# A third bank for scores, one bank for small jobs, and parts of maxima and tokens made by GpSimd, in a one-layer transformer kernel

## The chip, the cores and the metric

The kernel runs on one core of one Trainium2 chip. The metric is the device time of one execution in microseconds (us), lower is better. Several executions are timed and the median is given; one more execution is profiled.

## What is computed

The input x has 8 batches of 256 tokens of width 128 (2048 tokens). One layer in float32, normalised after each half:

```python
# attention: 16 heads of width 8
Q, K, V = proj(Wq, bq), proj(Wk, bk), proj(Wv, bv)
scores = einsum('bhqd,bhkd->bhqk', Q, K) / sqrt(8)
attended = einsum('bhqk,bhkd->bhqd', softmax(scores), V)
x = layernorm(x + attended @ Wo + bo)
# shared part (256 hidden) and 8 experts (128 hidden), the best 2 of 8 for each token
shared_out = (silu(xf @ sw1) * (xf @ sw3)) @ sw2
s = sigmoid(xf @ router_w.T)
_, topk_idx = top_k(s + router_bias, 2)      # gates: s of the chosen over their sum
routed_out = sum over the chosen e of gate_e * (gelu(xf @ ew1[e]) @ ew2[e])
x = layernorm(x + shared_out + routed_out)
```

## The kernel before

**Slots.** `lay_out_slots` writes the order of the work out by hand as a list of slots, and every engine runs through the same list, taking from each slot what is its own; semaphores tie the engines together. A slot holds up to one half-slot of scores (`s`), one of maxima (`m`), products with v (`pv`) and a list of small `jobs`. There are 14 slots of entry, 64 with scores, and a tail with 40 units. A batch takes eight half-slots; maxima run 12 slots ahead of scores.

**Attention.** In each half-slot TensorE makes the scores of two heads' tiles, keys by queries, for `r` = 0 and 1 (`scores`, L800), and the same products the other way round for two other tiles (`maxima`, L809). Scores and maxima use different 32-row groups of the array and are issued by turns. VectorE reduces each maxima bank to the largest score of each query (`top`, L672; three banks `max_bank`). When a batch's eight half-slots are reduced, `top` is negated and split in a high and a low part (`top_parts`, L681 and L682), TensorE transposes them (job "shift", L893, one slot later), ScalarE copies them (L618) and sends them by DMA (L621) into spare rows of `qstack`, so that the scores of that batch come out with the maximum subtracted. ScalarE takes the exponential of each scores bank (L570), TensorE multiplies with v (L826), and ScalarE copies the result (L578).

**Projections.** Queries and keys come in units of 512 tokens. The jobs "k" and "q" of unit n are a matmul (L882), two copies on ScalarE (L607, L611), a subtraction on GpSimd (L486), and 12 DMA copies each ("store", L371). "v" is L885. Unit 0 is made in another way in the entry (jobs "first").

**The small jobs of a batch.** "norm" (transposes L901, divided by the sums on VectorE, L702 and L703), "attT" (L907, copied by ScalarE, L624), "wo" (L912, added and its statistics taken on VectorE, L711 to L718), "y" (normalised on GpSimd, L496 to L499), "yT" (L918; ScalarE makes the high part `yt_hi`, L626, VectorE the low part `yt_lo`, L722), "router" (six small matmuls, exponential L630). Every second batch the group of 512 tokens is routed: route0 to route5 on GpSimd, with "sig", "rank" and "den" (L732 to L734) on VectorE between them, then "combT" (transposes L931, copy L636, DMA to scratch) and "load gates" (a DMA that spreads 2 MB to `gates_mem`). On GpSimd also stand "add bo" (L492) and 16 pieces of "split w" (L468, L470).

**The tail.** Unit u is three matmuls of 512 columns (L780 to L782), an activation (L643 or L645), a product with the gates (L750) or two for a shared unit (L742, L745), and two slots later the second matmul "down" (L960).

**PSUM banks.** There are eight of 512 columns: `ring` x2 (scores and units, used by turns), `max_bank` x3, `pv_bank`, `misc_bank` and `sum_bank`. Small jobs take `misc_bank` and `sum_bank` by turns:

```python
            banks = ([misc_bank, sum_bank] if n < tail else [misc_bank, max_bank[2]] if n < tail + 3
                     else [misc_bank, pv_bank, max_bank[2]] if n < tail + 14 else [misc_bank, pv_bank])
```

`wait_ring` makes TensorE wait, before it writes a ring bank, for the exponential of the bank's last use; `wait_bank` and `wait_taken` make it wait for the engine that reads a small job's bank.

## Time and profile before

| | |
|---|---|
| median of 3 runs | 232.85 us (232.33 to 233.04) |
| profiled execution, its own time | 230.98 us |
| its span, first to last instruction | 229.2 us |
| TensorE busy | 207.9 us, 91% of the span |
| VectorE busy | 157.3 us, 69% |
| ScalarE busy | 137.9 us, 60% |
| GpSimd busy | 107.5 us, 47% |
| mean granted TensorE clock | 0.974 of full |

The shares are means over stages with different limits: up to about 30 us the entry, to 121.5 us scores beside maxima, to 141 us scores alone, then the units. The lines named are those of the kernel before. PE is TensorE's matmuls, PEld its weight loads, DVE VectorE, ACT ScalarE, POOL GpSimd, SP the queue that issues most DMAs.

### The profile page before, as it was taken

The numbers are of one execution on the slowest core, as the hardware profiler recorded it, in microseconds if no ns is written. First come the engines' busy times: TensorE is split into PE (matmuls) and PEld (weight loads), VectorE is DVE, ScalarE is ACT, GpSimd is POOL, SyncE is SP. The second block draws the span as 40 slices with busy tenths as digits, with TensorE's granted clock in tenths as the row PEclk, the third lists the DMA queues.
The fourth block names the chain that finished last, engine by engine and source line by source line (L and its number), as shares of the span: only waits on it lengthen the run. The fifth ranks groups of instructions, "written<-read, shape, count | busy, mean of one in ns | idle before, by whom it ended". The sixth has DMA issues, their size and how long they took to land.

```text
span 229.2 us, 4496 instructions
## 1 busy us (share of the span) xinstructions
PE 207.9 (91%) x1538; PEld 120.0 (52%) x1538; DVE 157.3 (69%) x333; ACT 137.9 (60%) x280; POOL 107.5 (47%) x208
## 2 busy tenths in 40 slices
PE   7998979989998989999899999899998999999970
PEld 7764555435564645546454554466664455645520
DVE  6688877849899899989994030664548655556654
ACT  2899464878877778778778877334341533534330
POOL 8787997023506379582965156144003802020203
PEclk9999955999999999999999999999999999999998
DMA  4391654384410000009000350000090010541011
GB/s 154 107 258 31 167 166 104 99 307 104 103 27 6 3 6 4 9 3 366 10 3 6 140 233 0 3 1 0 3 366 0 3 47 1 182 186 46 3 44 48
DMA packets 10422, 19.19 MB, mean 84 GB/s; under 512 B 1952, under 2 KB 7008, under 8 KB 9760
## 3 DMA queue, kind: packets, MB, share of 16 engines
q1 hardware_dynamic: 8976, 17.06, 22.7%
q10 hardware_dynamic: 1040, 1.05, 1.3%
q0 software_dynamic: 384, 0.79, 1.3%
q8 instruction: 13, 0.21, 0.4%
q14 instruction: 9, 0.07, 0.1%
HBM read 12.80 MB, written 1.11 MB: 61 GB/s over the span
## 4 chain that ended last, share of the span: by engine, by line
PE 68%; DVE 18%; ACT 7%; issue 4%; ACTq 1%; POOL 0%; POOLq 0%; DVEq 0%
PE ring L800 14%; PE pv_bank L826 10%; PE max_bank L960 9%; DVE top L672 8%; PE sum_bank L960 4%; PE ring L782 3%; PE ring L780 3%; PE ring L781 3%; ACT probs_mem L570 3%; PE max_bank L809 3%; PE pv_bank L834 2%; DVE hid L750 2%; PE misc_bank L882 1%; ACT xt L645 1%; PE misc_bank L780 1%
## 5 line engine op out<-in xcount | busy, mean ns | idle before, releaser
L672 DVE TENSOR_REDUCE top<-max_bank 128x2 f32<-128x512 f32 x128 | 81.0, 682 | 10.7 <-PE max_bank L809 10.4
L570 ACT ACTIVATE probs_mem<-ring 128x512 f32<-128x512 f32 x128 | 70.0, 596 | 19.4 <-PE ring L800 17.8
L800 PE MATMUL ring<-qstack,kstack 32*128 32x256 f32 x256 | 45.5, 336 | 6.4 <-ACT probs_mem L570 3.7
L809 PE MATMUL max_bank<-kstack,qstack 32*128 32x256 f32 x256 | 44.4, 338 | 1.1 <-DVE top L672 0.8
L800 PEld LDWEIGHTS ring<-qstack,kstack 32*128 32x128 f32 x256 | 29.3, 190 | 27.1 <-ACT probs_mem L570 16.1
L826 PE MATMUL pv_bank<-probs_mem,v 128*18 128x256 f32 x512 | 41.4, 397 | 0.4 <-ACT probs_mem L570 0.4
L750 DVE TENSOR_TENSOR hid<-xt,gates_mem 128x512 f32<-128x512 f32 x32 | 22.5, 703 | 24.0 <-ACT xt L645 24.0
L645 ACT ACTIVATE xt<-ring 128x512 f32<-128x512 f32 x32 | 19.1, 598 | 32.4 <-PE ring L782 32.4
L960 PE MATMUL max_bank<-hid,wf 128*128 128x512 f32 x60 | 32.0, 614 | 1.7 <-DVE hid L750 1.4
L809 PEld LDWEIGHTS max_bank<-kstack,qstack 32*128 32x128 f32 x256 | 28.3, 190 | 5.9 <-POOL kstack L475 1.8
L780 PE MATMUL ring<-yt_hi,wf_lo 128*128 128x512 f32 x40 | 31.3, 782 | 0.0
L505 POOL TENSOR_SCALAR rstd<-mv 128x4 f32<-128x4 f32 (+1 forms) x5 | 1.9, 388 | 36.9 <-DVE mv L764 36.8
L782 PE MATMUL ring<-yt_hi,wf_hi 128*128 128x512 f32 x40 | 15.8, 395 | 0.0
L781 PE MATMUL ring<-yt_lo,wf_hi 128*128 128x512 f32 x40 | 15.8, 394 | 0.0
L826 PEld LDWEIGHTS pv_bank<-probs_mem,v 128*18 128x18 f32 x512 | 8.7, 97 | 9.9 <-issue 1.0
L960 PEld LDWEIGHTS max_bank<-hid,wf 128*128 128x128 f32 x60 | 9.6, 188 | 7.8 <-DVE hid L750 5.9
L486 POOL TENSOR_TENSOR gates_mem<-gates_mem 128x512 fp32r<-128x512 f32 x6 | 7.6, 1270 | 12.9 <-ACT gates_mem L611 12.9
L643 ACT ACTIVATE xt<-ring 128x512 f32<-128x512 f32 x8 | 4.8, 597 | 14.6 <-PE pv_bank L782 5.6
L499 POOL TENSOR_SCALAR xs<-res,mv,rstd 128x128 f32<-128x128 f32 x16 | 12.7, 802 | 0.9
L780 PEld LDWEIGHTS ring<-yt_hi,wf_lo 128*128 128x128 f32 x40 | 7.6, 190 | 9.5 <-issue 8.4
L781 PEld LDWEIGHTS ring<-yt_lo,wf_hi 128*128 128x128 f32 x40 | 7.6, 190 | 9.1 <-issue 9.1
L742 DVE SCALAR_TENSOR_TENSOR xt<-xt,ring 128x512 f32<-128x512 f32 x8 | 5.5, 688 | 9.1 <-ACT xt L643 9.1
(191 smaller groups left out, 333.2 us busy)
## 6 DMA issues: line engine op xcount, KB each, us to landing
gates_mem<-gate_scratch SPq DMA_DIRECT2D x4, 2048.0 KB, 7.2
kstack<-gates_mem SPq DMA_DIRECT2D x36, 64.0 KB, 2.1
qstack<-gates_mem SPq DMA_DIRECT2D x24, 64.0 KB, 2.1
wf<-w_ffn_dram SPq DMA_DIRECT2D x1, 1408.0 KB, 6.3
xs<-x_dram SPq DMA_DIRECT2D x4, 256.0 KB, 5.4
xt<-x_t_dram SPq DMA_DIRECT2D x3, 256.0 KB, 4.4
qstack<-gates_mem POOLq DMA_DIRECT2D x12, 64.0 KB, 2.3
out_dram<-xs SPq DMA_DIRECT2D x3, 256.0 KB, 2.3
```

The source lines that it names most:

```text
L499: ins = pool.tensor_scalar(xs[:, QT * n + t, :], res1[:, t, :], mv1[:, t, 0:1], rstd1[:, t:t + 1], ALU.subtract, ALU.mult)
L570: nc.scalar.activation(probs[:, i % 2, s_heads(s)[r], :], ring_of(("scores", 2 * s + r))[:, :], ACT.Exp, scale=SCALE).then_inc(probs_made, 1)
L645: nc.scalar.activation(act_out[:, b % 2, :], bank[:, :], ACT.Gelu).then_inc(act_made, 1)
L672: dve.tensor_reduce(top[:, m_heads(m)[r], t, :], max_bank[(2 * m + r) % NMAX][:, :].rearrange("p (h k) -> p h k", h=2), AX.X, ALU.max).the ...
L750: dve.tensor_tensor(hid[:, b % NHB, :], act_out[:, b % 2, :], gates_mem[:, g % 2, e * GT:(e + 1) * GT], ALU.mult).then_inc(hid_dve, 1)
L780: mm(out_ap, w_lo, m_hi, start=first, stop=False)
L781: mm(out_ap, w_hi, m_lo, start=False, stop=False)
L782: return mm(out_ap, w_hi, m_hi, start=False, stop=last)
L800: ins = mm(ring_of(("scores", 2 * s + r))[:, kt * S:(kt + 1) * S], kstack[rows, t, k:k + P], qstack[rows, t, b * S:(b + 1) * S], start=Tru ...
L809: ins = mm(max_bank[(2 * m + r) % NMAX][:, qt * S:(qt + 1) * S], qstack[rows, t, q:q + P], kstack[rows, t, b * S:(b + 1) * S], start=True, ...
L826: ins = mm(pv_bank[32 * j:32 * j + 2 * VW, 0:S], v[:, (QT * b + kt) * H // 2 + HPS * n + j, k * VW:(k + 2) * VW], probs[:, p // 2 % 2, j, ...
L960: mm(acc_bank[g][:, :], wf[:, c:c + P], hid[:, b % NHB, :], start=b == first_of(g), stop=b == last_of(g)).then_inc(down_made, 1)
```

## The change

1. **Scores in three banks.** Scores take `ring[0]`, `ring[1]` and `sum_bank` in turn. Units still take the two ring banks.
2. **Small jobs in one bank.** While there are scores, every small job uses `misc_bank`, and the layout spreads the jobs over slots of their own: "wo" goes a slot behind the shift, the router is cut in two jobs ("router0", "router") five and six slots later than before, "k", "q" and "v" of later units are moved.
3. **Parts of the maxima on GpSimd.** A job "tops", at the front of the slot in which a batch's last maxima are made, does with three operations what VectorE did with two. `top` has two copies.
4. **Parts of the tokens on GpSimd.** ScalarE copies the transposed tokens to `yt_raw`, GpSimd makes `yt_hi` and `yt_lo` from it; VectorE's L722 is gone.
5. **"combT" once for a group** (four transposes in one bank, one wider copy, one DMA). The second group's moves from slots 54 and 55 of the scores to the tail's first. The last group's routing starts one slot later (12 + n for 11 + n); its "combT" stays at 24.
6. **The third unit's queries** (unit 2) stand in slot 12 of the entry, before 13.
7. `hid`, the units' product, takes the place of half of the probabilities in SBUF.

```diff
@@ lay_out_slots
-                   (10, ("v", 0)), (11, ("k", 2)), (12, ("split rw", 0)), (13, ("q", 2))):
+                   (10, ("v", 0)), (11, ("k", 2)), (12, ("q", 2)), (12, ("split rw", 0))):
...
-    put(4, ("v", 2))
-    for n, job in ((8, ("k", 3)), (9, ("store", (3, 1))), (10, ("q", 3)), (12, ("store", (3, 0))), (13, ("v", 3))):
+    for n, job in ((2, ("v", 2)), (7, ("k", 3)), (8, ("store", (3, 1))), (15, ("q", 3)), (16, ("store", (3, 0))), (16, ("v", 3))):
...
+    for slot in slots:
+        if slot.m is not None and slot.m % 8 == 7:
+            slot.jobs.insert(0, ("tops", slot.m // 8))
...
-        for kind, n in (("norm", 2), ("attT", 3), ("wo", 4), ("y", 5), ("yT", 8)):
+        for kind, n in (("norm", 2), ("attT", 3), ("wo", 5), ("y", 6), ("yT", 9)):
             put(first + n, (kind, b))
         if b < NB - 2:
-            put(first + 9, ("router", b))
+            put(first + 14, ("router0", b))
+            put(first + 15, ("router", b))
         if b % 2:
             for kind, n in route:
-                put(first + 9 + n, (kind, b // 2))
+                put(first + 15 + n, (kind, b // 2))
             if b // 2 < 2:
-                put(first + 22, ("combT", b - 1))
-                put(first + 23, ("combT", b))
-                put(first + 25, ("load gates", b // 2))
+                put(first + 32, ("combT", b // 2))
+                put(first + 34, ("load gates", b // 2))
...
     for kind, n in route:
-        put(NHALF + 11 + n, (kind, NG - 1))
+        put(NHALF + 12 + n, (kind, NG - 1))
@@ banks
-            banks = ([misc_bank, sum_bank] if n < tail else [misc_bank, max_bank[2]] if n < tail + 3
+            banks = ([misc_bank, sum_bank] if n < first_s else [misc_bank] if n < tail else [misc_bank, max_bank[2]] if n < tail + 3
...
+                if use[0] == "scores":
+                    bank, n_scores = (ring + [sum_bank])[n_scores % 3], n_scores + 1
+                else:
+                    bank, n_units = ring[n_units % 2], n_units + 1
+                ring_of[use], ring_before[use], ring_latest[bank.name] = bank, ring_latest.get(bank.name), use
@@ GpSimd
+                    if kind == "tops":
+                        pool.wait_ge(max_taken, 16 * (n + 1))
+                        if n >= 2:
+                            pool.wait_ge(misc_made, made["shift", n - 2])
...
+                        chain(pool.tensor_scalar(hi, tops, -1.0, None, ALU.mult))
+                        chain(pool.tensor_scalar(tops, tops, -1.0, None, ALU.mult))
+                        pool.tensor_tensor(lo, tops, hi.bitcast(F32), ALU.subtract).then_inc(top_split, 1)
...
+                    if kind == "yT":
+                        wait_taken(pool, (kind, n))
+                        c = slice(n * S, (n + 1) * S)
+                        chain(pool.tensor_scalar(yt_hi[:, c], yt_raw[:, n % 2, :], 1.0, None, ALU.mult))
+                        pool.tensor_tensor(yt_lo[:, c], yt_raw[:, n % 2, :], yt_hi[:, c].bitcast(F32), ALU.subtract).then_inc(yt_made, 1)
@@ VectorE
-                    if m % 8 == 7:
-                        dve.wait_ge(max_taken, 2 * m + 2)
...
-                        chain(dve.tensor_scalar(hi, tops, -1.0, None, ALU.mult))
-                        dve.scalar_tensor_tensor(out=lo, in0=tops, scalar=-1.0, in1=hi.bitcast(F32), op0=ALU.mult,
-                                                 op1=ALU.subtract).then_inc(top_split, 1)
...
-                    if kind == "yT":
-                        dve.wait_ge(yt_hi_made, b + 1)
-                        dve.tensor_tensor(yt_lo[:, b * S:(b + 1) * S], misc[:, 0:S],
-                                          yt_hi[:, b * S:(b + 1) * S].bitcast(F32), ALU.subtract).then_inc(misc_dve, 1)
```

How the program stands before and after is shown in three places; a row is a source line, the instruction and its output and inputs. The new file's lines are numbered otherwise.

TensorE at the end of the entry, before; L882 to `misc_bank` is the third unit's queries, L800 the first scores:

```order
L809 MATMUL max_bank<-kstack,qstack 128x256 x4
L882 MATMUL sum_bank<-xt,wa 128x512
L809 MATMUL max_bank<-kstack,qstack 128x256 x8
L882 MATMUL misc_bank<-xt,wa 128x512
L800 MATMUL ring<-qstack,kstack 128x256
```

TensorE in the same place after, up to the second half-slot of scores (L896 was L882, L811 was L800, L820 was L809):

```order
L896 MATMUL sum_bank<-xt,wa 128x512
L820 MATMUL max_bank<-kstack,qstack 128x256 x4
L896 MATMUL misc_bank<-xt,wa 128x512
L820 MATMUL max_bank<-kstack,qstack 128x256 x4
L811 MATMUL ring<-qstack,kstack 128x256
...
L811 MATMUL sum_bank<-qstack,kstack 128x256
```

The queries' matmul has moved in front of four maxima, and the third scores bank is `sum_bank`.

GpSimd behind the DMA issues of the entry, before (L486 is the low part of keys or queries, L492 the addition of bo):

```order
L371 DMA qstack<-gates_mem 32x512 x12
L486 TENSOR_TENSOR gates_mem<-gates_mem 128x512
L461 TENSOR_SCALAR rw_parts<-rw 128x8
L462 TENSOR_TENSOR rw_parts<-rw,rw_parts 128x8
L486 TENSOR_TENSOR gates_mem<-gates_mem 128x512
L492 TENSOR_TENSOR xs<-xs,bo_all 128x512 x4
```

GpSimd in the same place after:

```order
L377 DMA qstack<-gates_mem 32x512 x12
L499 TENSOR_TENSOR gates_mem<-gates_mem 128x512 x2
L474 TENSOR_SCALAR rw_parts<-rw 128x8
L475 TENSOR_TENSOR rw_parts<-rw,rw_parts 128x8
L505 TENSOR_TENSOR xs<-xs,bo_all 128x512
L469 TENSOR_SCALAR top_parts<-top 128x4x8
L470 TENSOR_SCALAR top<-top 128x32
L471 TENSOR_TENSOR top_parts<-top,top_parts 128x4x8
L505 TENSOR_TENSOR xs<-xs,bo_all 128x512 x2
```

The parts of the second batch's maxima stand between the first addition and the next two.

TensorE around the shift of a batch in the middle, before:

```order
L826 MATMUL pv_bank<-probs_mem,v 18x256 x4
L893 MATMUL sum_bank<-ident,top_parts 32x128 x2
L912 MATMUL misc_bank<-wa,att_t 128x128 x2
L800 MATMUL ring<-qstack,kstack 128x256
L809 MATMUL max_bank<-kstack,qstack 128x256
```

The same place after, up to "wo":

```order
L837 MATMUL pv_bank<-probs_mem,v 18x256 x4
L907 MATMUL misc_bank<-ident,top_parts 32x128 x2
L811 MATMUL ring<-qstack,kstack 128x256
L820 MATMUL max_bank<-kstack,qstack 128x256
...
L837 MATMUL pv_bank<-probs_mem,v 18x256 x4
L926 MATMUL misc_bank<-wa,att_t 128x128 x2
```

The shift stands alone in its slot, and "wo" comes a slot later.

## Rows read from the trace of the kernel before

**Rows 1.** the page's first line, and TensorE's clock granted in 40 equal slices (tenths)
```profile
span 229.2 us, 4496 instructions
...
PEclk9999955999999999999999999999999999999998
```

**Rows 2.** windows of five stages: length, busy us (count) by engine, clock, DMA share, GB/s
```profile
29.30:39.60 10.30, 9.20 (x67) 5.49 (x68) 7.83 (x13) 5.83 (x12) 9.36 (x11) 0.51 0.48 127
39.60:54.50 14.90, 13.87 (x144) 6.71 (x144) 10.65 (x20) 11.98 (x24) 2.54 (x2) 1.00 0.60 185
54.50:121.50 67.00, 63.77 (x748) 35.58 (x746) 62.48 (x138) 52.61 (x112) 38.43 (x88) 1.00 0.15 50
121.50:141.00 19.50, 18.25 (x175) 9.54 (x171) 4.29 (x18) 14.93 (x33) 10.91 (x27) 1.00 0.27 111
141.00:229.20 88.20, 77.58 (x282) 45.20 (x280) 49.47 (x119) 32.17 (x58) 21.00 (x44) 0.99 0.17 61
```

**Rows 3.** groups by line, 54.5 to 121.5 us: busy, mean ns | idle before, releaser
```profile
L672 DVE TENSOR_REDUCE top<-max_bank 128x2 f32<-128x512 f32 x80 | 50.4, 680 | 1.5 <-PE max_bank L809 1.2
L570 ACT ACTIVATE probs_mem<-ring 128x512 f32<-128x512 f32 x79 | 43.4, 596 | 12.7 <-PE ring L800 11.4
...
L722 DVE TENSOR_TENSOR yt_lo<-sum_bank,yt_hi 128x256 fp32r<-128x256 f32 x5 | 2.1, 424 | 2.1 <-ACT yt_hi L626 2.1
...
L523 POOL TENSOR_SCALAR tie<-diff 128x256 f32<-128x256 f32 x2 | 1.7, 861 | 0.2
```

**Rows 4.** tile top_parts: duration ns min/median/max, first and last start
```profile
L681 DVE TENSOR_SCALAR top_parts<-top x8: 181/182/576, 21.8 to 121.1; 128x32 fp32r<-128x32 f32 x8
L682 DVE SCALAR_TENSOR_TENSOR top_parts<-top,top_parts x8: 191/192/1210, 22.3 to 121.4; 128x32 fp32r<-128x32 f32 x8
```

**Rows 5.** timeline around the shift of one batch: start us, us, instruction
```profile
66.40 0.68 DVE L672 TENSOR_REDUCE top<-max_bank 128x2 f32<-128x512 f32 x1
...
67.34 0.19 DVE L682 SCALAR_TENSOR_TENSOR top_parts<-top,top_parts 128x32 fp32r<-128x32 f32 x1
...
67.67 0.38 PE L893 MATMUL sum_bank<-ident,top_parts 128*32 128x128 f32 x2
```

**Rows 6.** timeline of the entry into the scores, 22 to 30 us
```profile
22.62 0.38 PE L893 MATMUL misc_bank<-ident,top_parts 128*32 128x128 f32 x2 [0.66 <-DVE top_parts L682]
...
28.77 0.68 ACT L611 ACTIVATE gates_mem<-misc_bank,wa 128x512 f32<-128x512 f32 x1
29.34 1.08 ACT L570 ACTIVATE probs_mem<-ring 128x512 f32<-128x512 f32 x2
...
30.00 0.58 PE L800 MATMUL ring<-qstack,kstack 32*128 32x256 f32 x1 [1.40 <-DVE top L672]
```

**Rows 7.** the chain that ended last, in order of time: start us, us, what
```profile
38.41 1.54 PE sum_bank L885 x8
...
47.08 0.68 ACT gates_mem L611
...
85.77 0.56 PE pv_bank L826 x8
87.29 0.56 PE pv_bank L826 x8
```

**Rows 8.** ACT's groups by line, 121.5 to 141 us
```profile
L570 ACT ACTIVATE probs_mem<-ring 128x512 f32<-128x512 f32 x24 | 13.1, 596 | 3.4 <-PE ring L800 3.0
```

**Rows 9.** timeline of the last group's routing, 190 to 193 us
```profile
190.06 0.23 POOL L537 TENSOR_SCALAR den_ok<-den 128x4 f32<-128x4 f32 x1 [2.79 <-DVE den_inv L734]
190.08 0.80 PE L780 MATMUL ring<-yt_hi,wf_lo 128*128 128x512 f32 x1
...
191.73 0.79 PE L780 MATMUL ring<-yt_hi,wf_lo 128*128 128x512 f32 x1
191.88 0.25 POOL L546 TENSOR_TENSOR comb<-picked,mask 128x32 f32<-128x32 f32 x1
...
192.83 0.38 PE L931 MATMUL misc_bank<-ident,comb 128*8 128x128 f32 x2
```

113 lines of the change are left out of this document (60 added, 53 removed).

## The prediction

> **What bounds the kernel now.** I read five stages first [rows 2]. From 54.5 to 121.5 us, where every slot makes one half-slot of scores, one of maxima and one product with v, VectorE is busy for 62.48 of 67.00 us, TensorE for 63.77 and ScalarE for 52.61. [...] Inside the stage [rows 3] the 80 reductions sit idle for only 1.5 us, and the piece of VectorE's time that is waste is 2.1 us in front of five yt_lo subtractions, which wait for ScalarE's yt_hi. ScalarE waits 11.4 us for scores: two ring banks make TensorE and ScalarE take turns. So VectorE is the bound here, with the turn-taking close behind. From 121.5 to 141 us there are no maxima; ScalarE is busy for 14.93 of 19.5 us and waits 3.0 us for scores [rows 2, 8]: the two banks are the limit there. From 141 us on are the 40 units, TensorE 77.58 of 88.2 us [rows 2]; a unit's slot costs 191.73 - 190.08 = 1.65 us [rows 9]. One more place stands out: the granted clock is 0.51 of full from 29.3 to 39.6 us, the lower of its two levels, and 1.00 or near it in the other four stages [rows 1, 2]. It fell while TensorE had just sat idle for 1.40 us at the entry into the scores [rows 6], behind ScalarE's two copies of the third unit's queries (28.77 + 0.68) and the first exponentials at 29.34.
>
> **The base of the sum.** The profiled execution took 230.98 us, 1.78 more than its span of 229.2 [rows 1]; the median shown is 232.85, so 1.87 above it. I make the sum against 230.98 and put it on the median unchanged.
>
> **Entry, 20 to 30 us.** The parts of the maxima of batch 0 go to GpSimd. The wait of TensorE before that shift was 0.66 us [rows 6]; I take GpSimd's step from six chained small operations, 190.06 to 191.88 + 0.25, so 2.07 / 6 = 0.345 us each [rows 9], and three of them are 1.04 against 0.18 + 0.19 and about 0.1 of chaining on VectorE [rows 4]. That is 0.6 us more in front of the shift, and some 0.2 for its place in GpSimd's queue: +0.8. Against it, the queries' matmul now stands before the last lone maxima, so ScalarE's two copies (0.68 each [rows 6]) end before the first scores rather than after them, and the second half-slot of scores finds the third bank free instead of waiting for an exponential. Of the 1.40 us of idle time almost all goes: -1.4. Together -0.6. Bounds: +0.8 (the copies are late anyway) and -1.4.
>
> **Clock, 29.3 to 39.6 us.** Four slots, bo, one v (1.54 us at the low level [rows 7]) and one shift fill 9.9 us. At full clock, slots in the middle of the kernel stand 87.29 - 85.77 = 1.52 us apart [rows 7], the v costs half of 1.54 to all of it, say 1.1, bo and shift 0.5 together: 4 x 1.52 + 1.6 = 7.7, a gain of 2.2 if the clock holds. I think it does, since the idle time that preceded the fall goes away. If it falls in the same place all the same, what is left is the shift there: VectorE's two parts took 0.58 and 1.21 us, the longest of their kinds [rows 4], beside GpSimd's additions; three GpSimd steps and half of one addition in its queue ahead of them (0.6) are about as long, so 0 to -0.8. The Trainium skill (TensorE: Matmul & The Clock Gate, "What's actually happening") says that the low level is the default and recent activity is what releases it. By that rule a fuller entry keeps the clock, which is the -2.2; the trace agrees in that the fall followed the idle time, but it shows four busy slots at the low level too, which the rule alone does not explain.
>
> **39.6 to 54.5 us.** The fourth unit's queries leave this stage for slot 15. Their two copies on ScalarE are 2 x 0.68, and the chain ran through such a copy at 47.08 [rows 7]: -1.4. The third bank covers some of the keys' copies: -0.2. Together -1.6, bounds 0 (they only move on) and -2.5.
>
> **54.5 to 121.5 us, five batches.** Removed from VectorE per batch: 0.18 + 0.19 + 0.42 = 0.79 us of work [rows 3, 4], 3.95 in all, and the 2.1 us of waits before yt_lo. That leaves 67.0 - 3.95 - 2.1 = 60.95. Given back: in the batch shown the last reduction ended at 66.40 + 0.68 = 67.08, VectorE's second part at 67.53, and TensorE came to the shift at 67.67, having waited for nothing [rows 5]. GpSimd will have them at 67.08 + 0.05 + 1.04 = 68.17, so TensorE stands 0.5 us, and VectorE, which then runs out of maxima, with it: 5 x 0.5 = 2.5. The later queries and v put some 0.3 here. 60.95 + 2.8 = 63.8: -3.2. Bounds: -6.05 (cover holds) and 0. GpSimd pays per batch three small steps (1.04) and two passes over 128x256; the nearest row for such a pass is 0.86 us [rows 3], so at most 1.04 + 1.72 = 2.8, or 14 us on top of 38.43 of 67 [rows 2]. That is 78% busy, and the tokens' parts are wanted only five slots later, so I cost them at nothing; if the cover goes, a batch costs up to 1.7 us. One bank for all small jobs costs nothing as long as each job's copy is done one slot (1.5 us) later, which copies of 0.4 to 0.7 us allow.
> The Trainium skill (SBUF — State Buffer, "SBUF: two separate sides") speaks against moving work to GpSimd: a GpSimd operation and a VectorE operation that reads two SBUF tensors exclude each other. Here the second part, which reads two, stretched from 0.19 to 1.21 us once [rows 4]. By that rule the new GpSimd work would slow VectorE, but the reductions read one tensor, in PSUM, so by rule and row alike the sum stays.
>
> **121.5 to 141 us.** Of the 3.0 us that ScalarE waits for scores [rows 8] the third bank takes 2.2, since TensorE can then make one exponential's scores ahead; what stays is behind small jobs. -2.2, bounds 0 and -3.4.
>
> **141 us on.** The last group's routing is put one slot later, its transposes are not. Before, the weights were ready at 191.88 + 0.25 = 192.13 and TensorE reached the transposes at 192.83: 0.70 us of slack [rows 9]. A slot is 1.65 us, so TensorE will wait 0.95. The second group's four transposes come into this stage; a pair takes 0.38 [rows 9], so +0.45 with overlap. Their wider copy stands before the first unit's activation: +0.3. Together +1.7, bounds +0.4 and +2.7.
>
> **Sum.** -0.6 - 2.2 - 1.6 - 3.2 - 2.2 + 1.7 = -8.1. 230.98 - 8.1 = 222.9 for the profile, 232.85 - 8.1 = 224.8 for the median.
>
> **Rivals.** (1) The clock falls all the same. GpSimd's parts make a wait of about 0.66 + 0.8 = 1.5 us before batch 0's shift, as long as the idle time that preceded the fall before. In the same place it costs 1.4 us of the sum, 226.2; earlier, up to 3 more, 229. Against it: the two idle pieces of before (0.66 and 1.40) become one. (2) The freed VectorE buys little, because the single bank and GpSimd's queue tie the engines together: the stage with maxima gives 0.5, the one after it 1.0, the tail costs 2.5, the rest as summed (-0.6 - 2.2 - 1.0): -2.8, or 230.0. For it speaks that TensorE too is shown 63.77 of 67. (3) Slower: the parts of the maxima come out of GpSimd's queue so late that TensorE stands long in every batch. It decides from about 1.7 us a batch on, since seven batches x (1.7 - 0.5) eat the 8.1, or from 1.3 us if such a wait makes the clock fall once more (2.2). Behind the two passes of the tokens' parts it would be 1.72 and, with one fall, 232.85 - 8.1 + 7 x 1.22 + 2.2 = 235.5. Against it: the tokens' parts stand two slots ahead in GpSimd's order. (4) Nothing changes: gains in the maxima stage only lengthen waits elsewhere, 232.8.
>
> **Chances.** The sum as it stands 0.50 (its own range 222.5 to 226.5), (1) 0.25, (2) 0.13, (4) 0.04, (3) 0.08. About 0.3% is what a measurement of this kernel can tell from no change. Faster 0.88, same 0.04, slower 0.08. The range goes from 221.5, where VectorE's cover holds, to 230.5, which takes in (1) and (2).
>
> **What would show it.** Right: granted clock 1.00 from 29 to 40 us; VectorE busy near 58.5 in a stage of about 64 us, TensorE waiting some 0.5 us before each shift; ScalarE's wait for scores after the maxima under 1 us; TensorE idle for 1 us before the last group's transposes. Wrong: a low clock stretch of the same or greater length; waits before the shift over 1.5 us; a stage after the maxima still at 19 us, which would mean that TensorE's own time was its limit.

## The result, and the profile after

The changed kernel is slower. Its median is 242.33 us (235.80 to 244.08, 6 executions), that of the kernel before 232.84 us (232.28 to 233.38, 6 executions): 9.5 us, or 4.1%, more. The forecast was 224.8, with a range of 221.5 to 230.5.

Executions of one and the same kernel differ in how long TensorE's granted clock stays at its lower level; left to the executions with the least of it, the ratio is still 1.019 (interval 1.0127 to 1.0252). To compare kernels I take from every execution its time at the low level, 2 x (1 - granted clock) x span. In 14 further executions of the kernel before, a straight line through the times rises by 0.33 us for each us at the low level, and passes 10 us at 230.7. The six of the changed kernel have 19.6 to 51.3 us of it. Their line, extended down to 10 us, where none of them lies, gives 233.9, which is 3.2 more. Set beside single executions of the kernel before with as much of it, the changed kernel is 2 to 3 us slower where both have 19 to 23 us, and 0.3 to 1.1 us slower where both have 44 us. So of the 9.5 us **some 3 at most are there at an equal clock**, and the rest comes with more time at the low level (44 us in the middle executions, about 16 in those of before).

The page of the changed kernel, its first line and the granted clock in 40 slices, to be held against [rows 1]:

```profile
span 242.2 us, 4497 instructions
...
PEclk9999959999999998557999555599999999999996
```

One low stretch has become three. The windows of the same kernel (columns as in [rows 2]) are cut at the shifts of successive batches; the first is the idle time before the shift at 95.21, the last three are the last shift to the first unit, the low stretch that begins in it, and the units:

```profile
93.80:95.20 1.40, 0.11 (x4) 0.02 (x1) 0.72 (x2) 0.48 (x1) 1.15 (x5) 0.97 0.00 0
68.12:81.33 13.21, 12.26 (x149) 6.71 (x150) 11.69 (x23) 10.12 (x22) 8.24 (x18) 1.00 0.04 13
81.33:95.21 13.88, 12.26 (x148) 6.70 (x149) 11.94 (x24) 10.13 (x22) 9.75 (x24) 1.00 0.01 4
95.21:113.78 18.57, 18.36 (x149) 8.88 (x149) 12.21 (x27) 10.11 (x22) 13.66 (x33) 0.54 0.01 3
127.34:152.99 25.65, 25.39 (x174) 12.53 (x175) 4.06 (x16) 14.01 (x30) 12.28 (x26) 0.60 0.09 35
132.80:156.60 23.80, 23.80 (x141) 11.36 (x142) 3.19 (x12) 13.40 (x28) 7.26 (x17) 0.50 0.03 8
152.99:242.20 89.21, 79.16 (x284) 46.30 (x282) 50.13 (x118) 32.92 (x57) 30.07 (x59) 0.96 0.22 83
```

The kernel before, cut at the same places:

```profile
67.67:80.97 13.30, 12.57 (x153) 6.96 (x150) 12.39 (x27) 10.44 (x23) 6.12 (x13) 1.00 0.01 4
80.97:94.33 13.36, 12.59 (x150) 6.99 (x149) 12.67 (x30) 10.41 (x23) 11.14 (x26) 1.00 0.01 4
94.33:108.32 13.99, 13.22 (x156) 7.22 (x153) 12.85 (x29) 11.01 (x25) 7.47 (x19) 1.00 0.39 153
121.70:140.98 19.28, 18.03 (x172) 9.49 (x171) 4.12 (x16) 14.73 (x32) 10.89 (x27) 1.00 0.27 113
140.98:229.20 88.22, 77.60 (x282) 45.22 (x281) 49.47 (x119) 32.17 (x58) 21.02 (x44) 0.99 0.17 61
```

The two batches that both kernels ran at full clock took 13.21 and 13.88 us after, 13.30 and 13.36 before. VectorE's work did fall, from 12.39 to 11.69 us in a batch, and bought 0.09 us in one and -0.52 in the other. The batch from 95.21 us took 4.6 us more than its counterpart and the stage after the maxima 6.4 more; those are the places with a clock of 0.54 and 0.60.

What took VectorE's gain are the waits of TensorE for the parts of the maxima. Around an ordinary shift (timeline; to be held against [rows 5]):

```profile
80.07 0.63 PE L837 MATMUL pv_bank<-probs_mem,v 128*18 128x256 f32 x8
80.18 0.29 POOL L469 TENSOR_SCALAR top_parts<-top 128x32 fp32r<-128x32 f32 x1 [0.74 <-DVE top L692]
80.56 0.29 POOL L470 TENSOR_SCALAR top<-top 128x32 f32<-128x32 f32 x1
80.93 0.25 POOL L471 TENSOR_TENSOR top_parts<-top,top_parts 128x32 fp32r<-128x32 f32 x1
81.33 0.38 PE L907 MATMUL misc_bank<-ident,top_parts 128*32 128x128 f32 x2 [0.63 <-POOL top_parts L471]
82.20 0.69 DVE L692 TENSOR_REDUCE top<-max_bank 128x2 f32<-128x512 f32 x1 [0.90 <-PE max_bank L820]
```

And around the one at which the clock fell, where GpSimd was in the middle of a group's routing:

```profile
92.94 1.04 POOL L534 TENSOR_TENSOR diff<-sel 128x64 f32<-128x64 f32 x4
94.07 0.29 POOL L469 TENSOR_SCALAR top_parts<-top 128x32 fp32r<-128x32 f32 x1
...
94.81 0.25 POOL L471 TENSOR_TENSOR top_parts<-top,top_parts 128x32 fp32r<-128x32 f32 x1
...
95.21 0.59 PE L907 MATMUL misc_bank<-ident,top_parts 128*32 128x128 f32 x2 [1.30 <-POOL top_parts L471]
...
96.59 0.69 DVE L692 TENSOR_REDUCE top<-max_bank 128x2 f32<-128x512 f32 x1 [2.07 <-PE max_bank L820]
```

In the first, GpSimd starts behind the last reduction it needs and takes three steps of 0.37 to 0.4 us. In the second nothing waits in front of L469: GpSimd comes to it from four `diff` operations, and the wait doubles. The wait at the entry is 1.54 us, the last shift's 0.94. The transpose at 95.21 already runs at the low level: its two take 0.59 us, 0.38 at 81.33. The list of waits (engine, line, releaser: total us, times, longest):

```profile
PE misc_bank L907 <- POOL top_parts L471: 6.5, 8, 1.5
...
PE pv_bank L948 <- POOL comb L564: 1.6, 1, 1.6
...
DVE top L692 <- PE max_bank L820: 22.4, 34, 2.4
```

VectorE's wait for maxima has grown from 10.4 us in the kernel before to 22.4. In the two batches at full clock it is 1.4 and 1.2 us, where it was 0.3 and none: the bank that VectorE empties is filled later, because the shift stands in TensorE's order ahead of the next maxima. In the batch at the low clock it is 5.3 us, with TensorE itself slower.

### The profile page after: what moved, and what is told of

The parts are those of the page before. It is cut to its first block, busy times and chain, and to the rows that moved or that the text cites. A ratio compares the mean times of both kernels' runs of the same rounds, so it can differ in the third digit from the quotient of the medians.

```text
span 242.2 us, 4497 instructions
## 1 busy us (share of the span) xinstructions
PE 219.4 (91%) x1538; PEld 123.2 (51%) x1538; DVE 152.2 (63%) x309; ACT 137.2 (57%) x276; POOL 128.5 (53%) x248
## 4 chain that ended last, share of the span: by engine, by line
PE 62%; ACT 13%; DVE 12%; POOL 6%; issue 5%; ACTq 1%; POOLq 0%; DVEq 0%
PE pv_bank L837 12%; PE max_bank L979 8%; PE ring L811 6%; DVE top L692 5%; PE sum_bank L979 4%; ACT probs_mem L588 3%; PE ring L789 3%; PE ring L791 3%; PE ring L790 3%; PE sum_bank L811 3%; ACT probs_mem L616 3%; ACT probs_mem L613 2%; PE pv_bank L845 2%; PE misc_bank L915 2%; DVE probs_mem L759 1%
## 5 line engine op out<-in xcount | busy, mean ns | idle before, releaser
L692 DVE TENSOR_REDUCE top<-max_bank 128x2 f32<-128x512 f32 x128 | 81.3, 684 | 22.5 <-PE max_bank L820 22.4
L588 ACT ACTIVATE probs_mem<-ring 128x512 f32<-128x512 f32 x86 | 49.3, 601 | 19.9 <-PE sum_bank L811 9.4
L837 PE MATMUL pv_bank<-probs_mem,v 128*18 128x256 f32 x512 | 48.1, 454 | 2.0 <-ACT att_raw L596 1.7
L759 DVE TENSOR_TENSOR probs_mem<-xt,gates_mem 128x512 f32<-128x512 f32 x32 | 23.3, 728 | 31.9 <-ACT xt L665 31.9
L820 PE MATMUL max_bank<-kstack,qstack 32*128 32x256 f32 x256 | 41.5, 353 | 0.7 <-DVE top L692 0.4
L811 PE MATMUL ring<-qstack,kstack 32*128 32x256 f32 x172 | 40.3, 372 | 1.2 <-DVE top L692 1.1
L979 PE MATMUL max_bank<-probs_mem,wf 128*128 128x512 f32 x60 | 32.1, 616 | 1.7 <-DVE probs_mem L759 1.4
L811 PEld LDWEIGHTS ring<-qstack,kstack 32*128 32x128 f32 x172 | 24.9, 217 | 12.0 <-ACT probs_mem L588 5.5
L588 ACT ACTIVATE probs_mem<-sum_bank 128x512 f32<-128x512 f32 x42 | 25.1, 599 | 7.5 <-PE ring L811 6.1
L820 PEld LDWEIGHTS max_bank<-kstack,qstack 32*128 32x128 f32 x256 | 26.1, 201 | 6.0 <-POOL kstack L488 1.9
L811 PE MATMUL sum_bank<-qstack,kstack 32*128 32x256 f32 x84 | 24.1, 372 | 0.2 <-DVE top L692 0.2
L811 PEld LDWEIGHTS sum_bank<-qstack,kstack 32*128 32x128 f32 x84 | 14.6, 216 | 6.3 <-issue 3.6
L518 POOL TENSOR_SCALAR yt_hi<-yt_raw 128x256 fp32r<-128x256 f32 x8 | 6.9, 856 | 19.4 <-ACT yt_raw L646 19.4
L979 PEld LDWEIGHTS max_bank<-probs_mem,wf 128*128 128x128 f32 x60 | 9.6, 188 | 8.1 <-DVE probs_mem L759 6.0
L512 POOL TENSOR_SCALAR xs<-res,mv,rstd 128x128 f32<-128x128 f32 x16 | 13.1, 826 | 0.9
```

The costliest lines, as they stand in the source:

```text
L512: ins = pool.tensor_scalar(xs[:, QT * n + t, :], res1[:, t, :], mv1[:, t, 0:1], rstd1[:, t:t + 1], ALU.subtract, ALU.mult)
L588: nc.scalar.activation(probs[:, i % 2, s_heads(s)[r], :], ring_of["scores", 2 * s + r][:, :], ACT.Exp, scale=SCALE).then_inc(probs_made, 1)
L692: dve.tensor_reduce(top[:, b % 2, m_heads(m)[r], t, :], max_bank[(2 * m + r) % NMAX][:, :].rearrange("p (h k) -> p h k", h=2), AX.X, ALU.m ...
L759: dve.tensor_tensor(hid[:, b % NHB, :], act_out[:, b % 2, :], gates_mem[:, g % 2, e * GT:(e + 1) * GT], ALU.mult).then_inc(hid_dve, 1)
L811: ins = mm(ring_of["scores", 2 * s + r][:, kt * S:(kt + 1) * S], kstack[rows, t, k:k + P], qstack[rows, t, b * S:(b + 1) * S], start=True, ...
L820: ins = mm(max_bank[(2 * m + r) % NMAX][:, qt * S:(qt + 1) * S], qstack[rows, t, q:q + P], kstack[rows, t, b * S:(b + 1) * S], start=True, ...
```

## The experiments

Twelve kernels were run, and three more for a point that was open. All made from the changed kernel except e2. The numbers of all of them, with the time at the low level of each execution and, where the executions spread enough, where their line passes 10 us:

```
kernel                              median   low-level us of each        at 10 us   ratio to before
before, beside e1 to e4 (14)        233.12   11.9 to 44.6                230.7
before, beside e5 to e8 (7)         233.89   12.4 to 40.7                230.6
before, beside e9 to e12 (7)        232.10   11.9 to 19.0                230.1
before, beside e13 to e15 (7)       233.08   16.1 to 40.7                230.7
changed                             242.33   19.6 23.1 44.2 44.3 51.3 x2   233.9    1.019 (1.013-1.025)
e1 parts of maxima on VectorE       231.89   11.8 x2, 34.6 x2            227.5      0.980 (0.971-0.989)
e2 before, parts on GpSimd          236.68   8.4 to 41.5 (10 executions) 235.1      1.012 (1.006-1.018)
e3 changed, matmuls before shifts   240.44   7.4 27.2 28.6 31.7          234.4      -
e4 e1, parts of tokens on VectorE   229.22   8.6 9.5 13.6, 34.2 x2       228.6      0.982 (0.972-0.992)
e5 changed, shift a slot later      238.54   14.1 29.4 49.2 49.4         228.1      -
e6 e1, two matmuls in 12 slots      231.81   10.1 x2, 11.1 13.0          231.5      1.000 (0.990-1.009)
e7 e1, last routing a slot sooner   226.69   9.4 x2, 9.9, 33.0           226.7      0.975 (0.966-0.984)
e8 e1, two banks for scores         239.34   17.8 35.5 38.0 38.1         234.1      -
e9 e7, matmuls at the entry         227.08   9.5 9.9 11.7, 32.9          226.6      0.979 (0.972-0.985)
e10 e9, one matmul in 12 slots      228.08   8.6 x2, 9.0 11.8            228.3      0.985 (0.979-0.990)
e11 e7, shift a slot later          235.16   15.4 35.6 x2, 39.1          227.4      -
e12 parts on GpSimd, shift later    234.87   6.3 32.1 34.1 x2            227.8      -
e15 e12, one matmul in 12 slots     231.11   10.4 14.2 17.0 18.0         228.9      0.987 (0.977-0.998)
```

A dash stands where no ratio was formed. The extra matmuls of e3, e6, e9, e10, e12, e14 and e15 write into a bank before its real contents are made, or into one that is idle, so they change only the time, and so does the repeated reduction of e13. The slopes of the lines that the column at 10 us is read from lie between 0.20 and 0.40 us for each us; e6, whose four executions lie between 10.1 and 13.0 us, is read at 10.1 instead.

That column is an estimate of unequal worth. The changed kernel, e5, e8, e11 and e15 have no execution as low as 10 us, so their lines are extended, and e11's fits its four points only within some 2 us. Where it can be had, a batch at full clock between two shifts is the better measure:

```
                                    near 66 to 81 us, near 80 to 95 us
before                              13.30             13.36
changed                             13.21             13.88
e8 two banks for scores             13.24             13.19
e4 all parts on VectorE             13.11             13.21
e11 maxima's parts on VectorE,
    shift later                     12.93             12.92
e1, e7 maxima's parts on VectorE    12.90             12.86, 12.87
e5, e12 parts on GpSimd,
    shift later                     12.70             12.69
```

### e1, e2: the parts of the maxima alone

The theory: GpSimd's parts hold TensorE before each shift. The rival: the new layout and the single small bank do it. e1 puts the parts back on VectorE in the changed kernel, e2 moves only them in the kernel before.

```diff
@@ e1, VectorE; the job "tops" is gone from GpSimd's list
+                    if m % 8 == 7:
+                        dve.wait_ge(max_taken, 2 * m + 2)
+                        if b >= 2:
+                            dve.wait_ge(misc_made, made["shift", b - 2])
...
+                        chain(dve.tensor_scalar(hi, tops, -1.0, None, ALU.mult))
+                        dve.scalar_tensor_tensor(out=lo, in0=tops, scalar=-1.0, in1=hi.bitcast(F32), op0=ALU.mult,
+                                                 op1=ALU.subtract).then_inc(top_split, 1)
```

> The changed kernel with the parts of the maxima made by VectorE again (two operations behind a batch's last reduction), all else as changed. Theory A (GpSimd's late parts make TensorE stand 0.6 to 1.5 us before each shift, VectorE idles behind it, and the granted clock falls): no wait before a shift over 0.3 us, low clock only in one stretch of about 7 to 10 us at the entry, 226 to 229 us. Rival B (the third bank and the single bank for small jobs do it: small jobs wait on one bank, and the clock falls for that): waits before the other small jobs stay, low clock still 30 us or more, 234 us or more.

> The kernel before with nothing but the parts of the maxima moved to GpSimd. A: waits of 0.5 us or more before the shifts, more low clock than the one stretch of 10.2 us, 236 us or more. B: GpSimd's parts are harmless, 231 to 234 us and one low stretch.

At 10 us of low clock e2 rose from 230.7 to 235.1, both with executions there: in the old layout the move costs 4.4 us. But four of its ten executions have only 8.4 to 8.9 us at the low level, and take 234.6 to 235.0, so it costs that much without one more fall of the clock, which I had not expected. In the new layout e1 is at 227.5, 6.4 us below the extended line of the changed kernel; against the changed kernel's own two executions at 19.6 and 23.1 us of low clock it is 5 to 6. Without the move the rest of the change is worth about 3 us. Windows between shifts of e1, then of e2:

```profile
65.59:78.49 12.90, 12.61 (x149) 7.00 (x150) 12.02 (x26) 10.23 (x23) 7.63 (x15) 1.00 0.05 14
78.49:91.35 12.86, 12.62 (x148) 6.98 (x149) 12.24 (x27) 10.17 (x23) 7.63 (x17) 1.00 0.02 4
```

```profile
68.86:82.57 13.71, 12.56 (x148) 6.94 (x149) 12.01 (x26) 10.37 (x22) 6.97 (x17) 1.00 0.01 4
82.57:97.00 14.43, 12.79 (x148) 7.08 (x149) 12.44 (x29) 10.45 (x22) 11.97 (x30) 1.00 0.01 4
```

Half of e1's executions had some 23 us more at the low level, which was not expected either. In the profiled one that is a stretch from 124.3 to 148.2 us, behind the maxima, so the shifts are not the only place where the clock falls.

### e3: keep TensorE busy while it waits

```diff
@@ TensorE, before the shift of each batch
+                        for _ in range(5):
+                            mm(misc[:, 0:P], ident[:, :], ident[:, :], start=True, stop=True)
                         pe.wait_ge(top_split, b + 1)
```

> The changed kernel with five extra 128-column matmuls of the identity into the small jobs' bank in front of each shift (some 1.1 us of TensorE work that is overwritten), so that TensorE works while GpSimd makes the parts. A, with the clock as the main price: the low stretches after the entry go or shrink to under 10 us in all, 230 to 234 us. If the waits cost by themselves and the clock fell for another reason: low clock as in the changed kernel (about 48 us), 242 us or more.

No shift waits any more, and the profile has no low stretch at the entry or at the shifts, where the changed kernel had two. But the five take 1.38 us in a place where the wait was 0.63, and the batches took 13.74 and 13.80 us. At 10 us of low clock e3 is at 234.4, no better than the changed kernel's 233.9, and its median, 240.44, is far above the 230 to 234 expected, since the stretch behind the maxima stayed. It ties the first two clock falls to idle time of TensorE, and gains nothing.

```profile
PEclk9999999999999999999998555699999999999996
```

### e4, e8: the tokens' parts, and the third bank

```diff
@@ e8
-                    bank, n_scores = (ring + [sum_bank])[n_scores % 3], n_scores + 1
+                    bank, n_scores = ring[n_scores % 2], n_scores + 1
```

> The changed kernel with the parts of maxima and of tokens both on VectorE as before: third bank, single bank, layout, one combT and earlier queries alone. A: 227 to 230 us, within 1.5 us of the kernel with only the maxima's parts back, one low stretch. B: 234 us or more with several low stretches.

> The kernel with the maxima's parts on VectorE, and scores in the two ring banks by turns again; layout, single bank and the tokens' parts as changed. If the third bank gives the gain: 230 us or more at about 10 us of low clock, ScalarE waiting over 10 us for scores in the stage with maxima. If the removed VectorE work gives it: 227 to 228.5 us. If the third bank is also what makes the stage without maxima fall to the low clock, no run has the long stretch.

Tokens' parts back on VectorE cost 1.1 us (228.6 against 227.5; a batch takes 13.11 against 12.90, the next 13.21 against 12.86): that move was right. Scores in two banks, in this layout, cost 5.5 us in the execution with 17.8 us of low clock and 2.4 to 3.3 us in those with 35 to 38, against e1's line; the 6.6 us between the two lines at 10 us (234.1 against 227.5) come from extending e8's. A batch at full clock takes 0.33 us longer (13.24 against 12.90). ScalarE's wait for scores from 54.5 to 121.5 us is 11.4 us there, and 6.9 + 2.6 behind both kinds of bank in e1. So the third bank is a part of the change that earns something. It is not the cause of the clock falling behind the maxima either: e8 has that stretch too.

### e5: the shift one slot later

```diff
-        slot = next(n for n in range(len(slots)) if slots[n].m == 8 * b + 7) + 1
+        slot = next(n for n in range(len(slots)) if slots[n].m == 8 * b + 7) + 2
...
-        for kind, n in (("norm", 2), ("attT", 3), ("wo", 5), ("y", 6), ("yT", 9)):
+        for kind, n in (("norm", 2), ("attT", 3), ("wo", 4), ("y", 5), ("yT", 9)):
```

> The changed kernel with the shift one slot later and wo in the slot that the shift had; the parts stay on GpSimd. If only the wait before the shift matters (A), the waits there fall under 0.2 us in most batches, a batch takes 13.0 us or less instead of 13.2 to 13.9, and the time at about 10 us of low clock is near the 227.5 us of the kernel with the parts on VectorE (226 to 229). If work on GpSimd costs in another way (VectorE or ScalarE slowed by it), it stays at 232 us or more at that much low clock.

The waits before all shifts but the entry's (1.51) are gone, and the parts are still on GpSimd. The batches take 12.70 and 12.69 us, where the changed kernel took 13.21 and 13.88, and the extended line gives 228.1 at 10 us. That is the strongest single evidence: it is not GpSimd's work itself that costs, but that its reader stands only one slot behind it. The median, 238.54, is still bad, because the low stretches stayed. One begins at 103.9 us, 1.5 us after a wait that did not come from a shift:

```profile
100.83 0.25 POOL L552 TENSOR_TENSOR picked<-mask,sig 128x32 f32<-128x32 f32 x1
...
101.12 0.19 DVE L739 TENSOR_REDUCE den<-picked 128x4 f32<-128x32 f32 x1 [2.48 <-POOL picked L552]
...
102.44 0.35 PE L811 MATMUL ring<-qstack,kstack 32*128 32x256 f32 x1 [1.30 <-DVE top L692]
```

The routing on GpSimd is late, since it also makes the parts of the tokens and of wf, VectorE stands 2.48 us in its in-order list for it, the maxima behind it are not reduced, and TensorE stands 1.30 us. Whether this wait makes the clock fall is not shown: e8 and e11, with the maxima's parts on VectorE and no wait over 0.8 us there, have a stretch of 3.4 us from about 107 us too.

### e6, e9, e10: the clock

e6 adds two 128-column matmuls to each of the 12 slots in which scores stand without maxima; e9 adds three before the shifts of batches 0 and 1; e10 has those and one in each of the 12 slots.

```diff
@@ e6 with range(2), e10 with range(1)
+                if s is not None and m is None:
+                    pe.wait_ge(max_taken, 2 * NHALF)
+                    for _ in range(2):
+                        mm(max_bank[0][:, 0:P], ident[:, :], ident[:, :], start=True, stop=True)
@@ e9
+                        for _ in range(3 if b < 2 else 0):
+                            mm(misc[:, 0:P], ident[:, :], ident[:, :], start=True, stop=True)
```

> The kernel with the maxima's parts on VectorE, and two extra 128-column matmuls of the identity into an idle maxima bank in each of the 12 slots with scores and no maxima. If TensorE's light work there is what lets the clock fall (the stretch of 23.9 us from about 120 us on), no such stretch in any run, all runs within 1 us of each other, 226.5 to 229 us. If the clock falls for another reason, the stretch stays in about half of the runs and the median is 230 us or more.

> Parts of maxima on VectorE, last routing one slot sooner, and three 128-column identity matmuls ahead of the shift of the first two batches only, where TensorE stood 0.68 and 0.70 us. If the short stretch at the low clock at the entry (6.8 us in the profile of the kernel without these matmuls) hangs on those waits, it goes, and at 0.33 us for each us at the low clock the time falls by about 2 us, to 224.5 to 225.5 in the executions without the long stretch. If it hangs on something else, the time stays at 226.2 to 227, and executions near 234 come as before.

> The same with one further matmul in each of the 12 slots in which the scores stand alone. If one is enough to keep the clock there, all executions lie within 1 us of each other, with no long stretch, at 225 to 228 (two in each slot cost about 3.5 us). If one is too little, executions of 232 to 236 with a stretch of over 20 us at the low clock come up again.

With extra matmuls behind the maxima no execution of e6 (4), e10 (4) or e15 (4) has the long stretch; without them it comes in 2 of 4 (e1), 2 of 5 (e4), 1 of 4 (e7), 1 of 4 (e9), told by some 23 us more at the low level. The stage took 17.85 us in e7 and 19.83 in e10 at full clock, so one matmul a slot costs 2.0 us, and two cost about 4. With that e6 missed the 226.5 to 229 us expected, though the clock held. e7 then e10:

```profile
119.61:137.46 17.85, 17.34 (x175) 9.52 (x175) 3.95 (x16) 13.78 (x31) 11.47 (x25) 1.00 0.13 51
```

```profile
119.57:139.40 19.83, 19.56 (x197) 11.54 (x197) 3.94 (x16) 14.32 (x31) 11.61 (x26) 1.00 0.14 55
```

e9 is a miss for my theory of the entry: the waits of 0.68 and 0.70 us are gone and the stretch of 6.8 us came all the same; the time, 226.6 at 10 us of low clock, is that of e7. e3, with five matmuls before every shift, did not have it. Nor is the length of one wait enough: the changed kernel stood 1.54 us before the shift at 23.91, longer than the 1.40 us after which the clock fell in the kernel before, and ran at full clock until 30.4. What triggers the fall at the entry stays open.

### e7: the last routing one slot sooner

```diff
-        put(NHALF + 12 + n, (kind, NG - 1))
+        put(NHALF + 11 + n, (kind, NG - 1))
```

> The kernel with the maxima's parts on VectorE and the last group's routing one slot sooner, as before the change. The wait of 1.6 us before the last group's transposes goes; 1 to 1.6 us less at equal low clock, so 225.9 to 226.5 us at about 10 us of it. Rival: that wait only gives TensorE's time to the next one, under 0.3 us less.

The wait for the last group's gates (1.6 us in e1 too) is gone, and 0.8 us of it reaches the end: 226.7 against 227.5. This has the lowest median: 226.69 us, 0.975 of the kernel before (0.966 to 0.984), just above the 225.9 to 226.5 expected; e9, at 227.08, cannot be told from it. e10 is 1.4 us above it but has all four executions between 227.77 and 228.71, partly above the 225 to 228 expected.

### e11, e12, e15: GpSimd again, with the shift later

e11 is e7 with the shift later as in e5. e12 is the changed kernel with the shift later, the last routing sooner and five matmuls before the shift; the text of its expectation says before each shift, but the kernel run has them only before those of the first two batches. e15 is e12 with one matmul in each of the 12 slots.

> Parts of maxima on VectorE, last routing one slot sooner, and the shift one slot later (the output matmul takes its place). If the remaining waits of TensorE before the shift (0.68, 0.70 and 0.31) matter, they go, and the time is 225 to 226.5 in the executions without the long stretch. If VectorE's chain sets the batches' time, it is 226.2 to 227, or above, since the second part of the chain now starts later.

> Parts of maxima on GpSimd as in the changed kernel, the shift one slot later, the last routing one slot sooner, and five 128-column matmuls ahead of each shift. If all that GpSimd's parts cost is the wait that they put before the shift, this comes out with the kernels that have them on VectorE: 226.5 to 229 at 10 us of low clock. If GpSimd's own time is the cost (its queue, the routing behind it), it stays above 231.

> Parts of maxima on GpSimd, the shift one slot later, the last routing one slot sooner, five identity matmuls ahead of the first two batches' shifts, and one in each of the 12 slots in which the scores stand alone. If GpSimd's parts cost nothing once the shift comes later, and one matmul a slot keeps the clock after the maxima, all executions lie between 226 and 230 us. If the stretch at the low clock near 105 us, seen in both kernels with a later shift, is followed by a long one all the same, executions near 235 come up.

At 10 us of low clock e11 is at 227.4, a loose reading, and e12 at 227.8, with ten matmuls more. The batches at full clock tell them apart, e11 first:

```profile
68.52:81.45 12.93, 12.38 (x152) 6.77 (x148) 12.01 (x26) 10.00 (x23) 7.41 (x14) 1.00 0.01 4
```

```profile
67.18:79.88 12.70, 12.42 (x153) 6.80 (x149) 11.70 (x24) 10.06 (x23) 8.24 (x17) 1.00 0.02 6
```

With the shift later, the parts on GpSimd are the better place: VectorE has 0.31 us less to do, and the batch is 0.23 us shorter. At the end nothing of it is seen, since e12's stretch near 106 us (6.8 us at the low level) is longer than e11's (3.4). e12's best execution (226.62, 6.3 us at the low level) is among the fastest of all. e11 missed the 225 to 226.5 expected, and three of its four executions and three of e12's have the long stretch. e15 held the clock behind the maxima, as expected, and came out at 228.84 to 232.27, partly above the 226 to 230 expected: a stretch of 3.4 us near 106 us, behind the late routing, is still there.

### e13, e14: which engine sets the batch

The prediction took VectorE for the bound of the stage with maxima. Both kernels are e5 plus work on one engine alone; each was run once, for its profile (243.28 and 239.39 us, with long low stretches in both), and only a batch at full clock is compared.

```diff
@@ e13, VectorE: one reduction of each batch is made twice
+                        if b < 8 and m % 8 == 3 and r == 0:
+                            chain(dve.tensor_reduce(top[:, b % 2, m_heads(m)[r], t, :],
...
@@ e14, TensorE, before "wo"
+                        for _ in range(2):
+                            mm(misc[:, 0:P], ident[:, :], ident[:, :], start=True, stop=True)
```

> The changed kernel with the shift one slot later, plus one reduction of 0.68 us repeated in each batch on VectorE. Read at the full clock between the shifts near 66 and 91 us, where the batches without it took 12.70 and 12.69 us. Theory now: TensorE's own 12.4 to 12.6 us set the batch and VectorE, at 11.7 to 12.0 us, has 0.7 us to spare, so the batch stays at 12.70 to 12.9. Rival, the prediction's reading that VectorE sets it: it grows by all of it, to 13.4.

> The changed kernel with the shift one slot later, plus two 128-column identity matmuls in each batch on TensorE, ahead of the output matmul. Five such took 1.38 us, so two are about 0.5 us. Theory now, TensorE sets the batch: it grows by that, to about 13.2 us. Rival, VectorE sets it: it stays at 12.7 to 12.8.

The same batch in e5, e13 and e14 (windows, one fence for each):

```profile
66.20:78.90 12.70, 12.42 (x153) 6.80 (x149) 11.69 (x24) 10.06 (x23) 8.24 (x17) 1.00 0.03 8
```

```profile
70.20:83.31 13.11, 12.71 (x152) 6.99 (x149) 12.29 (x25) 10.09 (x23) 8.22 (x17) 1.00 0.01 4
```

```profile
66.92:80.08 13.16, 12.87 (x156) 7.25 (x152) 11.68 (x24) 10.06 (x23) 8.20 (x17) 1.00 0.01 4
```

Two matmuls on TensorE lengthen the batch by 0.46 us of their 0.5; one reduction of 0.68 us on VectorE lengthens it by 0.41. The first is what my theory expected. The second is between the two theories: VectorE is busy for 0.60 us more (12.29 against 11.69), and 0.41 of it reaches the batch. Taking work off it counts at a like rate: from e11 to e12 0.31 us less gave 0.23, from e4 to e12, both moves and the later shift together, 0.58 less gave 0.41. So both engines set a batch of 12.7 to 13.1 us, TensorE's work nearly in full and VectorE's at about 0.7.

## Why the prediction was wrong

Three steps failed: the gain from freeing VectorE was taken in full, GpSimd's queue was put at nothing, and the clock was forecast to hold.

**Waits of 0.5 us in a batch: the size was nearly right, the base it was put on was not.** TensorE's ordinary wait was 0.63 us, and e5 against the changed kernel shows what it costs, 13.21 - 12.70 = 0.51. But I had put it on 60.95 / 5 = 12.19 us, VectorE's 13.4 less its 0.79 of work and 0.42 of waits, as if VectorE alone set the stage, although TensorE was shown busy for 63.77 of 67 us, more than VectorE. With no wait at all the batch is 12.70, with TensorE busy for 12.42. The two moves, with the later shift, were worth 0.41 us in the first of the two batches (e4 against e12), and 0.60 with the third bank and the layout (12.70 against 13.30), not the 1.21 of the sum: VectorE's work counts at about 0.7, and in place of its removed wait of 0.42 us it waits elsewhere (idle for 0.91 us of the batch before, for 1.01 in e5).

**GpSimd's place in its queue, costed at nothing, was the term that decided.** I took "three steps behind the last reduction". In 81.33:95.21 four routing operations stood ahead, the wait was 1.30, and the batch cost 13.88 - 12.69 = 1.19 us. I had looked at the tokens' parts in front of it and not at the routing. Rival (3) had named this queue, and priced it for waits of 1.7 us in each batch, or 1.3 with a fall of the clock.

**The entry (-0.6) held, and the clock fell all the same.** The wait before the first shift was 1.54 us, where 1.46 was forecast, and the 1.40 us of idle time at the second half-slot of scores shrank to 0.30. So that half-slot started at 29.37, where it had started at 30.00: -0.63. The second shift comes 1.4 us later than before, but that is the order of the jobs: the third unit's v now stands ahead of it, and stood behind it before. TensorE before, then after:

```profile
37.83 0.58 PE L893 MATMUL misc_bank<-ident,top_parts 128*32 128x128 f32 x2 [0.41 <-DVE top_parts L682]
38.21 1.74 PE L885 MATMUL sum_bank<-wa,xt 128*128 128x128 f32 x8
39.88 0.38 PE L800 MATMUL ring<-qstack,kstack 32*128 32x256 f32 x1
```

```profile
29.37 0.38 PE L811 MATMUL ring<-qstack,kstack 32*128 32x256 f32 x1 [0.30 <-DVE top L692]
...
33.83 2.08 PE L899 MATMUL misc_bank<-wa,xt 128*128 128x128 f32 x8
...
39.23 0.38 PE L907 MATMUL misc_bank<-ident,top_parts 128*32 128x128 f32 x2 [0.63 <-POOL top_parts L471]
39.54 0.38 PE L811 MATMUL ring<-qstack,kstack 32*128 32x256 f32 x1
```

Behind both jobs the scores go on at 39.54, before at 39.88. From the second half-slot to there it is 10.17 us, where it was 9.88: +0.3 for the -2.2 of the sum. The idle time that I held to be the cause of the fall was gone, and the clock fell at 30.4 us nevertheless.

**The clock term had the wrong sign.** The forecast was that the low stretch of 10.2 us would go (-2.2). It shrank to 6.8 us, and two new ones came. The stretch from 95.1 us begins in the wait of 1.30, TensorE busy for 0.11 of the 1.40 us before it; e1, without that wait, and e3, with it filled, do not have it. That is close to the mechanism of rival (3), a wait of 1.3 us and one more fall, with 0.08 given to it; but the wait came in one batch of seven, not in each. The stretch after the maxima is another thing. It comes in some executions of kernels whose last shift waits for 0.3 us at most, and matmuls added to those slots prevent it. The price used, 2.2 us a fall, was too small as well: the batch with 17 us at the low level took 18.57 us (14.42 in e1), the stage with 20 took 25.65 (17.85 in e7), so 4.2 and 7.8 us.

The Trainium skill (TensorE: Matmul & The Clock Gate, "What's actually happening") says that the moment of the change depends on where the kernel lands against the chip's own observation, so that the same program measures differently. The runs agree in that the same program differs: e1 had 11.8, 11.8, 34.6 and 34.6 us at the low level in four executions. That this is the reason, no run here shows. I had drawn only on its rule that activity releases the clock, for the -2.2.

**39.6 to 54.5 us (-1.6)** was mostly time moved on, which the bound of 0 had named. To the third shift the changed kernel took 13.38 us from 39.54 where the one before took 14.33 from 39.88, -0.95 with a wait of 0.62 in it, and e1 took 12.72: -1.6. But the fourth unit's queries then stand behind the third shift, and from there to the fourth it is 15.20 us (14.84 in e1), where it was 13.46. The sum had 0.3 for that.

**121.5 to 141 us (-2.2)** was right in kind: at full clock e7 takes 17.85 us where the kernel before took 19.28, -1.4, and the third bank as a whole is worth 2.4 to 5.5 us in this layout (e8). In the profiled execution the clock buried it: 25.65 us.

**141 us on (+1.7)** came out at 89.2 against 88.2, +1.0, of which its first 3.6 us at the low clock are a part. The wait I put at 0.95 was 1.6, and e7 shows that 0.8 us of it reaches the end.

**VectorE's freed time** was nearly right as a quantity, 12.39 - 11.69 = 0.70 us of work in a batch for the 0.79 forecast.

**A slip in rival (2).** It takes the stage from 39.6 to 54.5 us "as summed", but with -1.0 for the -1.6 of the sum; with -1.6 it gives 229.4 for 230.0, which changes nothing.

Added up from the profiles: -0.6 to the second half-slot of scores, +0.3 to the slot behind the second shift and the v, +0.8 to the fourth shift, +5.0 over the next three batches, +0.2 in the one after, +6.4 behind the maxima, +1.0 in the tail: +13.0 within rounding, the difference of the spans. That is +5.6 to the end of the stage with maxima, where the sum had -7.6, then +6.4 for its -2.2, and +1.0 for its +1.7.

## What to carry to other kernels

When two engines each show over 90% of a stage, neither is the bound alone: here a wait of 0.63 us on TensorE cost 0.51 us a batch, and 0.6 us of work put on VectorE or taken off it changed the batch by 0.4. Before a short chain is moved to a slower engine, read that engine's queue at every place where the chain will stand, and leave a slot between it and its reader: the same three GpSimd operations cost 0.3 and 1.0 us in a batch with their reader in the next slot, and saved 0.2 with one slot more. Before a stage is compared before and after, see that the same jobs lie between its two ends: the second shift came 1.4 us later only because a job had changed sides. A line through a few executions is good where they lie, and not beyond. Where a low clock can cost more than the edit gains, judge by several executions and by the time at each level, not by one profile.

## What the runs showed of the hardware

- Time at the lower clock level varies between executions of one kernel, here from 11.9 to 44.6 us in the kernel before and in visible steps (about 23 us more in e1, e4, e7 and e9), at about 0.33 us of time for each us.
- The clock fell in a stage in which the profile shows TensorE nearly always busy: in the changed kernel it was busy for 5.04 of 5.3 us before the fall near 132.7, with the 32-row matmuls of the scores and the 18-column ones with v:

```profile
127.40:132.70 5.30, 5.04 (x50) 2.95 (x50) 1.58 (x6) 3.56 (x8) 4.86 (x10) 1.00 0.41 164
```

  In e1 it was busy for 5.05 of 5.3 us (119.0 to 124.3) and the clock fell; in e7, the same program there, for 5.04 of 5.3 us (119.6 to 124.9) and it did not. One 128 x 128 matmul in each slot, or two, prevented it in 12 of 12 executions (e6, e10, e15). Whether their size or their number does it was not tried.
- Three chained GpSimd operations on 128x32 have their starts 0.37 and 0.38 us apart (80.18, 80.56, 80.93), at durations of 0.25 to 0.29, and TensorE starts 0.15 us after the last one ends. VectorE made the same parts in two operations of 0.18 and 0.19 us [rows 4].
- One of the eight executions of the kernel before in the last session took 584.94 us where the others took 231.9 to 241.7. It is in no comparison and not explained.
